# A gated cross-attention block on one core: the last five steps get an instruction order of their own, and TensorE adds the head products of the last tiles

## The chip, the cores and the metric

The kernel runs on one core of a Trainium2 chip. The metric is the device time of one execution in microseconds. Five engines work side by side, each through its own list of instructions in program order, and they wait for each other through semaphores: TensorE (PE, with its weight loads PEld), VectorE (DVE), ScalarE (ACT), GpSimd (POOL) and SyncE (SP), which here only issues transfers.

## What is computed

For 32 sequences of 56 rows with 128 features, in fp32:

```
x = x + tanh(g_xattn) * attention(layernorm(x), ctx[:, :56])   # 16 heads of 64, causal
h  = rmsnorm(layernorm(x)) ; q, k, v per row: 16 heads of 8
att = softmax_g(q[h] . k[g] / sqrt(8))      # among the 16 heads of the same row
y  = layernorm(x) + (att @ v) @ Wo + bo
gate = softmax(rmsnorm(y) @ Wg + bg)        # 8 experts, all are computed
x = x + tanh(g_ffn) * (y + sum_e gate[e] * rmsnorm(y) @ We[e])
```

The causal mask lets no row see beyond key 56, so 56 of the 1500 context rows are used.

## The kernel before

The attention works on 16 pairs of sequences (112 rows). The second half works on 14 tiles of 128 rows, which don't line up with the pairs. A software pipeline of steps `t` joins them: step `t` does the attention of pair `t`, projects a quarter of the queries or keys of a later group (`PROJECT_AT`, steps 2 to 13), and works on up to three tiles: `fa`, whose rows have just become whole, `fb`, one step older, and `fc`, two steps older; POOL adds up the experts of a fourth, `fd`. `TILE_AT` says which tile starts at which step; step 9 starts none. Tile 11 starts in step 14, tile 12 in 15 and tile 13 in 16. There is no attention left from step 16 on, so steps 16, 17 and 18 hold only tiles 11 to 13 (and POOL's sums in step 19).

The order of the instructions on each engine is written out by hand, in one loop per engine (L311 POOL, L443 ACT, L623 DVE, L822 PE). On PE a step is: scores of pair `t` in `ps_b`, `new_y` (output projection of pair `t-1`), `turn_o(fc)`, `shift(t)` (subtracts the row maxima), `new_o(fc)`, four projections, `first(fa)` (tile `fa` into `ps_e`), `turn_x2(fc)`, `values`, `gate_logits(fc)`, `turn_probs(t)`, `expert_half(fc, 0)`, `attend(t)`, `expert_half(fc, 1)`. The expert products, `turn_o`, `new_o` and the gate logits share the two banks of `ps_c`.

Tile `fb` is the work of DVE and POOL: `products` multiplies queries and keys into `prod1` (16 x 16 x 8 values a row, POOL the first `HP` = 10 heads, DVE the other 6), `logits` on DVE adds them over 8 (L529), `shifted_logits` takes maximum and difference, ACT takes exponentials (`head_exps`), `weighted` multiplies them with the values into `prod2` (POOL `HQ` = 6 heads, DVE 10), `mixed_heads` adds over 16 (L554), `normed_heads` scales. For `fc` come `new_x2`, `squares` and `x2_copy` on ACT, gate logits, `gating` on POOL (L304), the expert products scaled on ACT (`experts`, eight instructions of 128 columns, L414), and four additions on POOL (`outputs`, L281 to L289), after which SP stores the tile.

Ahead of everything PE runs seven small products of the identity (L655), while the first loads are under way.

All PE products made through the helper `mm` carry its line, L658. An fp32 product is two MATMUL rows, a transpose or a bf16 product one.

Of the kernel before, what the change touches and what calls it, by code (L numbers as in the profile page):

```python
# [31 lines left out]
WARM_UP = 7  # L32
# [9 lines left out]

def first_step(f):

    return (128 * (f + 1) + T - 1) // T
# [3 lines left out]
LAST_STEP = first_step(NT - 1) + 2  # L49
PROJECT_AT = {t: [("qk"[t % 2], t // 2 + 1, n) for n in range(4)] for t in range(2, NP - 2)}  # L50
# [40 lines left out]
def build(nc, xp, x_t, ctx_t, wq, wk, wv, wo, fw, fup, fdn, fwe, out):  # L91
    with ExitStack() as stack:
# [6 lines left out]
        def sem(name):  # L99
# [89 lines left out]
            o_turned oT_ready o_made x2_ready ssq_ready r2_ready x2_turned x2T_ready  # L189
# [7 lines left out]
        def score_banks(p):  # L197
            return ps_c if p == 1 else ps_b

# [3 lines left out]
        def _(sp):  # L203
# [13 lines left out]
            for f in range(NT):  # L217
                sp.wait_ge(s["out_ready"], f + 1)
                sp.dma_start(out[f * 128:(f + 1) * 128, :], out_sb[f % 2][:, :]).then_inc(stored[f % 2], 16)
# [4 lines left out]
        def _(pool):  # L224
# [31 lines left out]
            def products(f):  # L256
                pool.wait_ge(s["qkv_ready"], f + 1)
                if f > 0:
                    pool.wait_ge(s["logit_ready"], f)
                t = fqkv[f % 2]  # L260
                nc.gpsimd.tensor_tensor(  # L261
                    prod1[:, 0:HP, :, :],
                    t[:, D:2 * D].rearrange("p (g d) -> p g d", g=FH).unsqueeze(1).to_broadcast([128, HP, FH, FD]),
                    t[:, 0:HP * FD].rearrange("p (h d) -> p h d", h=HP).unsqueeze(2).to_broadcast([128, HP, FH, FD]),
                    ALU.mult).then_inc(s["prod1_pool"], 1)

            def weighted(f):
                pool.wait_ge(s["e_ready"], f + 1)
                if f > 0:
                    pool.wait_ge(s["oraw_ready"], f)  # L270
                nc.gpsimd.tensor_tensor(  # L271
                    prod2[:, 0:HQ, :, :],
                    e_sb[f % 2][:, 0:HQ, :].unsqueeze(2).to_broadcast([128, HQ, FD, FH]),
                    fqkv[f % 2][:, 2 * D:3 * D].rearrange("p (d g) -> p d g", d=FD).unsqueeze(1).to_broadcast([128, HQ, FD, FH]),
# [31 lines left out]

            row_scales(0, 2, 1)
# [3 lines left out]
            for t in range(2, LAST_STEP + 2):  # L311
# [3 lines left out]
                if fd is not None:  # L315
                    outputs(fd)
                if fc is not None:
                    second_scale(fc)
                if t < NP:
                    norm(t)  # L320
# [4 lines left out]
                if fc is not None:  # L325
                    gating(fc)

        @block.scalar
        def _(act):
# [64 lines left out]
            def squares(f):  # L394
# [4 lines left out]
                nc.scalar.activation(exb[f % XB][:, E, :], x2[f % 2][:, 0:D], ACT.Copy, scale=gates[:, 2:3])  # L399
# [10 lines left out]
            def experts(f, half):  # L410
                act.wait_ge(s["gate_ready"], f + 1)
                act.wait_ge(s["hi_made" if half else "lo_made"], f + 1)
                for e in range(4 * half, 4 * half + 4):
                    last = nc.scalar.activation(exb[f % XB][:, e, :], ps_c[:, half, e % 4 * D:(e % 4 + 1) * D],  # L414
# [28 lines left out]
            for t in range(2, LAST_STEP + 1):  # L443
# [3 lines left out]
                if t < NP:  # L447
                    exps(t)
                if fc is not None:
                    squares(fc)  # L450
                for fill in PROJECT_AT.get(t, ()):
                    project(*fill)
# [4 lines left out]
                if t < NP:  # L457
                    values(t, 0)
# [10 lines left out]
                if fc is not None:  # L469
                    experts(fc, 0)  # L470
                if fa is not None:
                    kv_copy(fa)
                if fc is not None:
                    experts(fc, 1)

        @block.vector
        def _(dve):
# [40 lines left out]
            def products(f):  # L518
                dve.wait_ge(s["kv_copied"], f + 1)
                nc.vector.tensor_tensor(  # L520
                    prod1[:, HP:FH, :, :],
                    ps_e[:, f % 2, 2 * D:3 * D].rearrange("p (g d) -> p g d", g=FH).unsqueeze(1).to_broadcast([128, FH - HP, FH, FD]),
                    fqkv[f % 2][:, HP * FD:D].rearrange("p (h d) -> p h d", h=FH - HP).unsqueeze(2).to_broadcast([128, FH - HP, FH, FD]),
# [16 lines left out]
            def weighted(f):  # L540
                dve.wait_ge(s["e_ready"], f + 1)
                nc.vector.tensor_reduce(esum[f % 2][:, :], e_sb[f % 2][:, :, :], AX.X, ALU.add).then_inc(s["esum_ready"], 1)
                nc.vector.tensor_tensor(  # L543
                    prod2[:, HQ:FH, :, :],
                    e_sb[f % 2][:, HQ:FH, :].unsqueeze(2).to_broadcast([128, FH - HQ, FD, FH]),
                    ps_e[:, f % 2, 3 * D:4 * D].rearrange("p (d g) -> p d g", d=FD).unsqueeze(1).to_broadcast([128, FH - HQ, FD, FH]),
                    ALU.mult).then_inc(s["prod2_ready"], 1)

            def mixed_heads(f):
                dve.wait_ge(s["esum_ready"], f + 1)  # L550
                nc.vector.reciprocal(einv[f % 2][:, :], esum[f % 2][:, :]).then_inc(s["einv_ready"], 1)
                dve.wait_ge(s["prod2_ready"], f + 1)
# [23 lines left out]
            def gate_sum(f):  # L576
                dve.wait_ge(s["gexp_ready"], f + 1)
                nc.vector.reciprocal(ginv[f % 2][:, :], gsum[f % 2][:, :]).then_inc(s["ginv_ready"], 1)

# [43 lines left out]
            for t in range(2, LAST_STEP + 1):  # L623
# [5 lines left out]
                if t <= NP:  # L629
                    new_x1(t - 1)  # L630
                if fc is not None:
# [4 lines left out]
                if fb is not None:  # L636
                    logits(fb)
# [9 lines left out]
                if fb is not None:  # L647
                    mixed_heads(fb)
                    normed_heads(fb)

        @block.tensor
        def _(pe):
            pe.wait_ge(s["consts"], 2)
            for _n in range(WARM_UP):
                nc.tensor.matmul(ps_b[:, 0, 0:128], ident[:, :], ident[:, :], start=True, stop=True)  # L655
# [92 lines left out]
            def turn_o(f):  # L748
                pe.wait_ge(s["onorm_ready"], f + 1)
                if f > 0:  # L750
# [3 lines left out]
            def new_o(f):  # L754
                if f > 0:
# [142 lines left out]
```

## Time and profile before

| | |
|---|---|
| runs | 275.45, 276.04, 277.45 us; median 276.04 |
| the profiled execution's own time | 274.52 us |
| its span, first to last instruction | 272.5 us |
| PE busy | 240.0 us (88%) |
| DVE, ACT, POOL busy | 193.0, 169.7, 163.9 us |
| TensorE clock, mean granted | 0.947 of 2.4 GHz |

Span and profiled time differ by 2.0 us, which lie around the span. The profiled execution is 1.5 us under the median. In the trace, times are counted from the span's start; the two numbers at the start of a row are its start and its length in us, and what stands in brackets at its end is how long the engine had stood idle before it and what ended that.

### The profile page before, as it was taken

What the parts mean: (1) busy time and instruction counts of PE and PEld (TensorE: products, weight loads), DVE (VectorE), ACT (ScalarE), POOL (GpSimd) and SP (SyncE); (2) the same over time, 40 slices, a digit from 0 to 9 for tenths busy, and PEclk for the clock granted to TensorE, in tenths of its full rate; (3) what the DMA queues carried; (4) which work ended last, traced back from release to release, by engine and by line L of the source; (5) the groups of instructions that cost most, each with busy time, mean ns of one, the idle gap of its engine ahead of it and who ended that gap; (6) DMA issues with size and microseconds to landing.
All of it is one profiled execution on the core that took longest, in us unless ns stands there. A gap on an engine that the chain in (4) does not pass through costs nothing.

```text
span 272.5 us, 7694 instructions
## 1 busy us (share of the span) xinstructions
PE 240.0 (88%) x3146; PEld 169.4 (62%) x3146; DVE 193.0 (71%) x327; ACT 169.7 (62%) x502; POOL 163.9 (60%) x173
## 2 busy tenths in 40 slices
PE   7999979897999999999999999899999797843770
PEld 6765766767676675859585867586857374612320
DVE  0237543479798888888889714998889988998710
ACT  3546516483868768777776767657786555744431
POOL 4104042546476777868684538656877777898544
PEclk9999999999999999999999999999999889996555
DMA  6990000000000000000000000000000000000000
GB/s 196 362 301 9 0 4 2 4 0 5 0 2 10 2 13 4 10 2 12 4 2 10 2 11 2 12 2 0 5 10 2 12 5 11 2 10 10 0 10 10
DMA packets 6016, 7.28 MB, mean 27 GB/s; under 512 B 477, under 2 KB 4830, under 8 KB 5982
## 3 DMA queue, kind: packets, MB, share of 16 engines
q1 hardware_dynamic: 5550, 6.16, 7.1%
q10 hardware_dynamic: 432, 0.64, 0.7%
q8 instruction: 25, 0.41, 0.6%
q14 instruction: 9, 0.07, 0.1%
HBM read 5.88 MB, written 0.92 MB: 25 GB/s over the span
## 4 chain that ended last, share of the span: by engine, by line
PE 65%; ACT 13%; DVE 13%; issue 4%; POOL 2%; DMA 1%; POOLq 0%; SPq 0%; ACTq 0%; DVEq 0%
PE ps_a L658 36%; PE ps_c L658 12%; PE ps_b L658 8%; DVE ps_e L529 5%; ACT probs L359 5%; PE ps_b L710 3%; PE ps_e L658 3%; DVE psums L497 2%; DVE ps_e L554 2%; ACT exb L414 2%; DMA cT<-in_ctx_t 1%; ACT junk L398 1%; ACT qT L342 1%; POOL exb L281 1%; DVE prod L543 1%
## 5 line engine op out<-in xcount | busy, mean ns | idle before, releaser
L261 POOL TENSOR_TENSOR prod<-fqkv 128x1280 f32<-128x1280 f32 x14 | 40.7, 2906 | 3.4 <-DVE fqkv L515 1.9
L658 PE MATMUL ps_c<-fwe_sb,x2T 128*128 128x512 f32 x56 | 34.4, 710 | 5.6 <-DVE glog L571 5.6
L252 POOL TENSOR_TENSOR probs<-probs,prinv 120x672 f32<-120x672 f32 x16 | 22.8, 1427 | 23.8 <-DVE prinv L501 23.7
L414 ACT ACTIVATE exb<-ps_c,gate 128x128 f32<-128x128 f32 x112 | 32.5, 397 | 6.4 <-POOL gate L304 4.2
L658 PE MATMUL ps_a<-aT,wo_sb 128*128 128x112 f32 x256 | 32.9, 281 | 1.0 <-issue 0.6
L658 PEld LDWEIGHTS ps_a<-aT,wo_sb 128*128 128x128 f32 x256 | 29.9, 191 | 3.6 <-issue 1.5
L529 DVE TENSOR_REDUCE ps_e<-prod 128x256 f32<-128x2048 f32 x14 | 32.0, 2286 | 0.0
L281 POOL TENSOR_TENSOR exb<-exb 128x640 f32<-128x640 f32 x14 | 21.6, 1540 | 17.3 <-ACT exb L414 17.3
L554 DVE TENSOR_REDUCE ps_e<-prod 128x128 f32<-128x2048 f32 x14 | 31.3, 2239 | 0.0
L658 PE MATMUL ps_a<-wv_sb,cT 128*64 128x512 f32 x128 | 31.0, 605 | 0.0
L271 POOL TENSOR_TENSOR prod<-e_sb,fqkv 128x768 f32<-128x768 f32 x14 | 25.3, 1810 | 7.2 <-ACT e_sb L387 7.2
L658 PE MATMUL ps_a<-xT,wqc 128*128 128x224 f32 x128 | 27.7, 359 | 1.2 <-ACT qT L342 0.6
L353 ACT COPY aT<-ps_a 128x448 f32<-128x448 f32 x32 | 15.5, 535 | 21.0 <-PE ps_a L658 21.0
L658 PE MATMUL ps_a<-cT,wk_sb 128*128 128x224 f32 x128 | 27.6, 360 | 0.5
L492 DVE TENSOR_REDUCE nmax<-ps_b 120x16 bf16<-120x896 f32 x15 | 16.3, 1086 | 14.0 <-PE ps_b L658 13.9
L658 PEld LDWEIGHTS ps_a<-xT,wqc 128*128 128x128 f32 x128 | 23.1, 190 | 4.8 <-ACT qT L342 3.7
L658 PEld LDWEIGHTS ps_a<-probsT,v_sb 56*64 56x64 f32 x1024 | 17.2, 139 | 13.8 <-ACT probsT L366 12.9
L658 PEld LDWEIGHTS ps_a<-cT,wk_sb 128*128 128x128 f32 x128 | 23.1, 190 | 3.7 <-ACT kT L342 2.8
L342 ACT COPY kT<-ps_a 128x448 f32<-128x448 f32 x32 | 16.9, 530 | 10.5 <-PE ps_a L658 10.3
L497 DVE TENSOR_REDUCE psums<-probs 120x16 f32<-120x896 f32 x16 | 17.4, 1085 | 8.1 <-ACT probs L359 8.1
L658 PE MATMUL ps_a<-probsT,v_sb 56*64 56x56 f32 x1024 | 19.1, 225 | 3.8 <-ACT probsT L366 3.2
L348 ACT COPY v_sb<-ps_a 128x512 f32<-128x512 f32 x32 | 19.2, 598 | 5.3 <-PE ps_a L658 5.3
(122 smaller groups left out, 456.8 us busy)
## 6 DMA issues: line engine op xcount, KB each, us to landing
xp_sb<-in_xp SPq DMA_DIRECT2D x1, 896.0 KB, 8.0
out<-out_sb SPq DMA_DIRECT2D x14, 64.0 KB, 1.5
xT<-in_x_t SPq DMA_DIRECT2D x1, 784.0 KB, 9.5
cT<-in_ctx_t SPq DMA_DIRECT2D x1, 784.0 KB, 11.1
wv_sb<-in_wv SPq DMA_DIRECT2D x1, 512.0 KB, 8.0
wo_sb<-in_wo SPq DMA_DIRECT2D x1, 512.0 KB, 12.2
fwe_sb<-in_fwe SPq DMA_DIRECT2D x1, 512.0 KB, 9.0
fw_sb<-in_fw SPq DMA_DIRECT2D x1, 266.0 KB, 11.7
```

What stands on the lines that cost most here:

```text
L252: nc.gpsimd.tensor_tensor(pr[0:TG, NC:C, :, 0:S], pr[0:TG, NC:C, :, 0:S], prinv[p % 2][0:TG, NC:C, :].unsqueeze(3).to_broadcast([TG, C - N ...
L261: nc.gpsimd.tensor_tensor(prod1[:, 0:HP, :, :], t[:, D:2 * D].rearrange("p (g d) -> p g d", g=FH).unsqueeze(1).to_broadcast([128, HP, FH, ...
L271: nc.gpsimd.tensor_tensor(prod2[:, 0:HQ, :, :], e_sb[f % 2][:, 0:HQ, :].unsqueeze(2).to_broadcast([128, HQ, FD, FH]), fqkv[f % 2][:, 2 * D ...
L281: nc.gpsimd.tensor_tensor(x[:, 0:5, :], x[:, 0:5, :], x[:, 5:10, :], ALU.add).then_inc(s["sum5"], 1)
L342: nc.scalar.copy(dst[:, 2 * k:2 * k + 2, :], ps_a[:, b, 0:2 * GT].rearrange("p (c t) -> p c t", c=2)).then_inc(a_free[b], 1)
L348: nc.scalar.copy(v_sb[p % 2][:, bt, :, :], ps_a[:, b, :].rearrange("p (c d) -> p c d", c=C)).then_inc(a_free[b], 1)
L414: last = nc.scalar.activation(exb[f % XB][:, e, :], ps_c[:, half, e % 4 * D:(e % 4 + 1) * D], ACT.Copy, scale=gate[f % 2][:, e:e + 1])
L492: nc.vector.tensor_reduce(nmax[p % 2][0:TG, :, :], score_banks(p)[0:TG, :, 0:C * S].rearrange("p r (c k) -> p r c k", c=C), AX.X, ALU.max, ...
L497: nc.vector.tensor_reduce(psums[p % 2][0:TG, :, :], probs[p % 2][0:TG, :, :, 0:S], AX.X, ALU.add).then_inc(s["psum_ready"], 1)
L529: nc.vector.tensor_reduce(ps_e[:, f % 2, 0:2 * D].rearrange("p (h g) -> p h g", h=FH), prod1[:, :, :, :], AX.X, ALU.add).then_inc(s["logit ...
L554: nc.vector.tensor_reduce(ps_e[:, f % 2, 0:D].rearrange("p (h d) -> p h d", h=FH), prod2[:, :, :, :], AX.X, ALU.add).then_inc(s["oraw_read ...
L658: return nc.tensor.matmul(o, lhsT, rhs, start=start, stop=stop, skip_group_check=True)
```

## The change

1. The loops end before step 14 (`TAIL`). Steps 14 and 15 get a loop of their own with another order, and steps 16 to 18 are written out for tiles 11, 12 and 13 (`third`, `prior`, `last`).
2. For tiles 10, 11 and 12 PE does the work of `logits`: `logit_sums`, 8 fp32 products of the identity with a slice of `prod1`, 256 columns wide with a stride of 8 values, added up in PSUM. For tile 12 it also does the sum over `prod2`: `head_sums`, 16 products of 128 columns, stride 16. From tile 10 on the heads are shared 8 and 8 in `prod1` and POOL 5, DVE 11 in `prod2`.
3. The expert products of tiles 11 to 13 go to the free banks of `ps_b`, `ps_a`, `ps_b` and no longer wait for the gate logits.
4. The last tile is finished on DVE: gate, four scaled additions straight from PSUM for experts 4 to 7, and three additions, after ACT has scaled experts 0 to 3. POOL adds only the residual.
5. Four small products `stay_warm` on PE behind the gate logits of tile 12.
6. The seven small products at the start become one, 512 columns wide.
7. Steps 2 to 13 are reordered too: DVE does `logits` before `new_x2`, `prob_sums` and `norm`; ACT does the projection copies before `squares`, `head_exps` before both `values` copies, and `experts` 1 before 0; POOL does `norm` before `second_scale`; PE starts the bias half of `new_o` (`bias_o`) ahead of `shift`.

```diff
+TAIL = 14
+END = 16
+HP_LATE = 8
+HQ_LATE = 5
+PE_LOGITS = (10, 11, 12)
+PE_MIXED = (12,)
+BIG = {11: "b", 12: "a", 13: "b"}
+STAY_WARM = 4
@@ pool, steps below 14
-                if fc is not None:
-                    second_scale(fc)
                 if t < NP:
                     norm(t)
+                if fc is not None:
+                    second_scale(fc)
@@ vector
             def products(f):
+                hp = product_heads(f)[0]
                 dve.wait_ge(s["kv_copied"], f + 1)
+                if f - 1 in PE_LOGITS:
+                    dve.wait_ge(s["logit_ready"], f)
...
+            def last_experts(f):
+                x = exb[f % XB]
+                dve.wait_ge(s["last_base"], 1)
+                dve.wait_ge(s["gate_ready"], f + 1)
+                dve.wait_ge(s["hi_made"], f + 1)
+                for e in range(4, E):
+                    if e > 4:
+                        dve.wait_ge(s["last_acc"], e - 4)
+                    nc.vector.scalar_tensor_tensor(out=x[:, E, :], in0=expert_banks(f)[:, 1, (e - 4) * D:(e - 3) * D], scalar=gate[f % 2][:, e:e + 1],
+                                                   in1=x[:, E, :], op0=ALU.mult, op1=ALU.add).then_inc(s["last_acc"], 1)
...
-            for t in range(2, LAST_STEP + 1):
+            for t in range(2, TAIL):
...
+                if fb is not None:
+                    logits(fb)
                 if fc is not None:
                     new_x2(fc)
                 if t < NP:
                     prob_sums(t)
                     norm(t)
                 if fb is not None:
-                    logits(fb)
                     shifted_logits(fb)
...
+            last, prior, third = NT - 1, NT - 2, NT - 3
+            new_x1(NP - 1)
+            products(prior)
+            new_x2(third)
+            shifted_logits(prior)
+            scaled_qkv(last)
+            weighted(prior)
+            products(last)
+            gate_logits(third)
+            head_scales(prior)
+            logits(last)
+            shifted_logits(last)
+            normed_heads(prior)
+            gate_sum(third)
+            weighted(last)
+            new_x2(prior)
+            head_scales(last)
+            head_sums(last)
+            normed_heads(last)
+            gate_logits(prior)
+            gate_sum(prior)
+            new_x2(last)
+            gate_logits(last)
+            gate_sum(last)
+            last_gating(last)
+            last_experts(last)
+            last_sums(last)
@@ tensor
-            for _n in range(WARM_UP):
-                nc.tensor.matmul(ps_b[:, 0, 0:128], ident[:, :], ident[:, :], start=True, stop=True)
+            nc.tensor.matmul(ps_b[:, 0, :], ident[:, :], ident[:, :].unsqueeze(1).to_broadcast([128, 4, 128]), start=True, stop=True)
...
+            def logit_sums(f):
+                pe.wait_ge(s["prod1_ready"], f + 1)
+                pe.wait_ge(s["prod1_pool"], f + 1)
+                for d in range(FD):
+                    ins = mm(ps_e[:, f % 2, 0:2 * D], ident[:, :], prod1[:, :, :, d].rearrange("p h g -> p (h g)"),
+                             start=(d == 0), stop=(d == FD - 1))
+                ins.then_inc(s["logit_ready"], 1)
...
+            for t in range(TAIL, END):
+                fa, fb, fc = TILE_AT.get(t), TILE_AT.get(t - 1), TILE_AT.get(t - 2)
+                scores(t)
+                new_y(t - 1)
+                shift(t)
+                bias_o(fc)
+                turn_o(fc)
+                values(t, 0)
+                new_o(fc)
+                first(fa)
+                turn_x2(fc)
+                if fb in PE_LOGITS:
+                    logit_sums(fb)
+                gate_logits(fc)
+                values(t, 1)
+                turn_probs(t)
+                expert_half(fc, 1)
+                attend(t)
+                expert_half(fc, 0)
+
+            last, prior, third = NT - 1, NT - 2, NT - 3
+            new_y(NP - 1)
+            turn_o(third)
+            bias_o(third)
+            new_o(third)
+            first(last)
+            logit_sums(prior)
+            turn_x2(third)
+            expert_half(third, 1)
+            gate_logits(third)
+            head_sums(prior)
+            bias_o(prior)
+            turn_o(prior)
+            expert_half(third, 0)
+            new_o(prior)
+            turn_x2(prior)
+            expert_half(prior, 0)
+            gate_logits(prior)
+            stay_warm(prior)
+            bias_o(last)
+            turn_o(last)
+            new_o(last)
+            expert_half(prior, 1)
+            turn_x2(last)
+            gate_logits(last)
+            expert_half(last, 0)
+            expert_half(last, 1)
```

## Rows read from the trace of the kernel before

**Rows 1.** The page's slices: granted TensorE clock in tenths, 40 slices

```profile
PEclk9999999999999999999999999999999889996555
```

**Rows 2.** Busy time by stretch: length, then PE, PEld, DVE, ACT, POOL; clock, DMA

```profile
216.50:219.80 3.30, 3.30 (x54) 1.80 (x58) 3.17 (x7) 1.84 (x6) 2.74 (x3) 0.50 0.03 7
...
236.70:247.10 10.40, 4.38 (x18) 2.17 (x17) 9.53 (x16) 5.84 (x26) 9.28 (x11) 1.00 0.02 6
247.10:257.30 10.20, 6.43 (x13) 2.93 (x13) 9.07 (x13) 4.00 (x16) 6.11 (x8) 0.51 0.02 6
257.30:272.50 15.20, 6.46 (x12) 3.02 (x12) 0.90 (x4) 3.91 (x16) 7.20 (x10) 0.50 0.03 9
```

**Rows 3.** The chain that ended last, in a middle step

```profile
78.49 1.14 PE ps_b L658 x68
...
89.90 0.87 PE ps_c L658 x2
...
92.91 0.93 PE ps_b L658 x52
```

**Rows 4.** The timeline of the same step

```profile
82.39 3.58 PE L658 MATMUL ps_a<-cT,wk_sb 128*128 128x224 f32 x16
...
84.19 1.43 PEld L658 LDWEIGHTS ps_a<-cT,wk_sb 128*128 128x128 f32 x8 [0.47 <-ACT kT L342]
...
84.87 1.31 POOL L252 TENSOR_TENSOR probs<-probs,prinv 120x672 f32<-120x672 f32 x1
84.89 2.29 DVE L529 TENSOR_REDUCE ps_e<-prod 128x256 f32<-128x2048 f32 x1
...
88.77 0.90 PEld L710 LDWEIGHTS ps_b<-ident,probs 120*128 120x128 f32 x8
```

**Rows 5.** The timeline of the start

```profile
1.56 3.36 PE L655 MATMUL ps_b<-ident 128*128 128x128 f32 x14 [1.56 <-POOL ident L228]
...
4.96 3.49 PE L658 MATMUL ps_a<-cT,wk_sb 128*128 128x224 f32 x16
...
9.00 0.34 PEld L658 LDWEIGHTS ps_e<-wq_sb,cmat 128*128 128x128 f32 x2 [0.52 <-DMA wq_sb<-in_wq]
```

**Rows 6.** The timeline: where steps 14, 15 and 16 begin on PE

```profile
206.60 0.38 PE L658 MATMUL ps_b<-hide_b,ident_b 56*64 56x448 bf16 x4
...
221.24 0.38 PE L658 MATMUL ps_b<-hide_b,ident_b 56*64 56x448 bf16 x4
...
234.98 2.04 PE L658 MATMUL ps_a<-aT,wo_sb 128*128 128x112 f32 x16
```

**Rows 7.** The timeline of steps 16 to 19

```profile
247.14 0.41 PE L752 MATMUL ps_c<-ident,onorm 128*128 128x128 f32 x1 [3.38 <-DVE onorm L560]
...
252.40 3.78 PE L658 MATMUL ps_c<-fwe_sb,x2T 128*128 128x512 f32 x4 [1.78 <-DVE glog L571]
...
269.98 0.45 POOL L289 TENSOR_TENSOR out_sb<-exb 128x128 f32<-128x128 f32 x1
```

**Rows 8.** Groups of instructions: busy us, mean ns of one, idle before

```profile
L529 DVE TENSOR_REDUCE ps_e<-prod 128x256 f32<-128x2048 f32 x14 | 32.0, 2286 | 0.0
L554 DVE TENSOR_REDUCE ps_e<-prod 128x128 f32<-128x2048 f32 x14 | 31.3, 2239 | 0.0
L520 DVE TENSOR_TENSOR prod<-ps_e,fqkv 128x768 f32<-128x768 f32 x14 | 13.3, 948 | 0.0
L543 DVE TENSOR_TENSOR prod<-e_sb,ps_e 128x1280 f32<-128x1280 f32 x14 | 20.7, 1477 | 0.0
L537 DVE TENSOR_TENSOR ps_e<-ps_e,lmax 128x256 f32<-128x256 f32 x14 | 6.1, 432 | 0.5
L565 DVE SCALAR_TENSOR_TENSOR x<-xc,rstd,ps_c 128x128 f32<-128x128 f32 x14 | 4.9, 348 | 8.1 <-PE ps_c L658 8.1
L414 ACT ACTIVATE exb<-ps_c,gate 128x128 f32<-128x128 f32 x112 | 32.5, 397 | 6.4 <-POOL gate L304 4.2 <-PE ps_c L658 2.2
L281 POOL TENSOR_TENSOR exb<-exb 128x640 f32<-128x640 f32 x14 | 21.6, 1540 | 17.3 <-ACT exb L414 17.3
```

More of the change, by code:

```diff
@@ L326, in _ @@
                     gating(fc)
+            for t in range(TAIL, END):
+                fa, fb, fc, fd = (TILE_AT.get(t - k) for k in range(4))
+                products(fb)
+                outputs(fd)
+                norm(t)
+                second_scale(fc)
+                first_scale(fa)
+                weighted(fb)
+                gating(fc)
+            last, prior, third = NT - 1, NT - 2, NT - 3
+            products(prior)
+            outputs(third - 1)
+            first_scale(last)
+            second_scale(third)
+            weighted(prior)
+            products(last)
+            gating(third)
+            weighted(last)
+            second_scale(prior)
+            outputs(third)
+            gating(prior)
+            second_scale(last)
+            last_residual(last)
+            outputs(prior)
         @block.scalar
@@ L441, in _ @@
             attended(1, 1)
-            for t in range(2, LAST_STEP + 1):
+            for t in range(2, TAIL):
                 fa, fb, fc = (TILE_AT.get(t - k) for k in range(3))
@@ L469, in _ @@
                 if fc is not None:
[L470 removed]
+                    experts(fc, 1)
                 if fa is not None:
@@ L473, in _ @@
                 if fc is not None:
-                    experts(fc, 1)
+                    experts(fc, 0)
+            for t in range(TAIL, END):
+                fa, fb, fc = (TILE_AT.get(t - k) for k in range(3))
+                o_copy(fc)
+                values(t, 0)
+                exps(t)
+                x1_copy(fa)
+                squares(fc)
+                x2_copy(fc)
+                head_exps(fb)
+                values(t, 1)
+                turned_probs(t)
+                gate_exps(fc)
+                attended(t, 0)
+                attended(t, 1)
+                kv_copy(fa)
+                experts(fc, 0)
+                experts(fc, 1)
+            last, prior, third = NT - 1, NT - 2, NT - 3
+            o_copy(third)
+            x1_copy(last)
+            x2_copy(third)
+            squares(third)
+            head_exps(prior)
+            kv_copy(last)
+            gate_exps(third)
+            head_exps(last)
+            o_copy(prior)
+            experts(third, 1)
+            experts(third, 0)
+            squares(prior)
+            x2_copy(prior)
+            o_copy(last)
+            gate_exps(prior)
+            squares(last)
+            x2_copy(last)
+            experts(prior, 1)
+            experts(prior, 0)
+            gate_exps(last)
+            experts(last, 0)
         @block.vector
@@ L621, in _ @@
             nc.vector.tensor_scalar(fwe_sb[:, :, :], fwe_sb[:, :, :], g2_sb[:, 0:1], gates[:, 1:2], ALU.mult, ALU.mult).then_inc(s["experts_scaled"], 1)
-            for t in range(2, LAST_STEP + 1):
+            for t in range(2, TAIL):
                 fa, fb, fc = (TILE_AT.get(t - k) for k in range(3))
@@ L820, in _ @@
             attend(1)
-            for t in range(2, LAST_STEP + 1):
+            for t in range(2, TAIL):
                 fa, fc = TILE_AT.get(t), TILE_AT.get(t - 2)
```

148 lines of the change are left out of this document (116 added, 32 removed).

## The prediction

> **What bounds the kernel now.** I read the page's slices first, then the chain that ended last in a middle step, then its timeline, then the stretches at the end. The slices give the full clock nearly everywhere, a dip near the 31st and a fall in the last four [rows 1]. A middle step lasts 14.4 us from one set of scores to the next (78.49 to 92.91), and its chain is almost all PE [rows 3]: PE bounds steps 2 to 13. Steps 14 and 15 have no projection, which takes 3.4 us of PE's time [rows 4], yet last 14.6 and 13.7 us (206.60, 221.24, 234.98) [rows 6]: there DVE, which must bring the probabilities, the logits and the exponentials in one line, ends last. Of the 14.6, about 1 us is the clock: it was 0.50 from 216.5 to 219.8 [rows 2], when PE had just stood waiting for DVE. From 234.98 to POOL's last addition, which ends at 270.43 [rows 6, 7], three tiles run nearly one behind the other, with DVE busy 9.5 us of 10.4 and 9.1 of 10.2 in the first two rounds, but 0.9 of 15.2 in the last; PE is busy less than half of the time and its clock is 0.50 from 247 on [rows 2]. This tail is 35.4 us.
>
> The sum is made in the profiled execution: 272.5 us of span, 274.52 us in all. The median is 1.5 us above it; I carry the difference over to the median.
>
> **The start.** Fourteen rows of the warm-up take 3.36 us, about 0.24 each, and the sixteen of the keys behind them 3.49 us, 0.218 each for 224 columns [rows 5]. A row of 512 columns at the full clock takes half of 0.87 us, 0.435 [rows 3], which makes 0.11 for 128: so the warm-up ran at half the clock and the keys at the full one. The new product is two rows of 512, 1.7 us at half clock, and then PE stands idle until the first load is in, at 4.96. If the clock is still at half there, as I expect, the cost depends on how long. The stretch at 0.50 in rows 2 lasted 3.3 us of busy PE; such a stretch here costs half of itself, 1.6. All sixteen rows at half clock would cost 2.7 (0.17 more each). The second product of `wq_sb` waited 0.52 us for its load [rows 5], and that cover takes some away. I take +1.0, between 0 and +2.7.
>
> **Steps 2 to 13.** The third projection waits for ACT's copy, which stands behind `squares`; that costs PE 0.06 us a step (82.39 plus half of 3.49 is 84.13, and it starts at 84.19) [rows 4, 5]. Moving the copies forward takes this away, ten times: -0.5. On the other side DVE's `logits`, 2.29 us, now stands ahead of the probability sums and the norm. POOL's norm started at 84.87, after `second_scale`, which now comes behind it. By my walk `logits` runs from 82.1 to 84.4, `new_x2` to 84.7, the sums and reciprocal to 86.1, and the norm on POOL, up to 1.5 us beside DVE's, to 87.7. The transposes of the probabilities start at 88.77 [rows 4], so 1.1 us of cover is left. `squares`, moved behind the copies, hands `x1_copy` on 0.3 us later, and the probability copies start when PE has made them, as before. `new_x2` comes 2.1 us later, with its transposition only 4 us behind the old one on PE; `bias_o` delays the exponentials by 0.2 us, beside the projections. I take -0.5, between -1 and +0.5; if the cover is gone, every late us of the norm is one on PE, in ten steps (a rival below).
>
> **Steps 14 and 15.** DVE loses 2.29 us of `logits` (L529) a step; its share of products grows from 768 to 1024 columns and from 1280 to 1408, 0.3 and 0.15 us more by L520 and L543 [rows 8]; POOL's share shrinks by as much work. PE gains 16 rows of 256 columns. Half a row of 512 is 0.217 [rows 3]; by the key rows with 224 columns it is 0.25 [rows 5]. That is 3.5 to 4.0 us a tile. PE's own work in such a step is 14.4 less 3.4 for the projections, 11.0 at most, and 10.5 if the small gaps of the middle step close: with the sums 14.0 to 15.0. So PE becomes the bound again and fills what DVE leaves. Against 14.6 and 13.7 the two steps give -0.3 to +1.6; I take +0.2, the end without gaps, since PE then never idles long and the 1 us of low clock should go. The added waits of DVE for `logit_ready` of the tile before are met a step early. `values` ahead of `new_o` and the first copy ahead of `exps` hold the exponentials back to 5.5 us into the step; norm and transposes still meet, since `logit_sums` covers PE until 9.5.
>
> **The tail.** Counted from the start of `new_y(15)`: 1.95 us of it, then tile 11's `new_o` behind ACT's last experts, then `first(13)`, and `logit_sums(12)` can start at 3.95 and end near 8.0, ready for DVE. Then DVE has one unbroken line: difference and maximum of tile 12 (0.9), exponentials (0.5), sums and product (2.0), product of tile 13 (1.2), gate and reciprocal (0.6), `logits(13)` 2.3, maximum and difference 0.9, `onorm(12)` and small ones 0.4, sums and product of 13 (2.0), `new_x2(12)` 0.35, reciprocal, L554 2.24, `onorm(13)`: 13.9 us, to 21.9 by the sizes of L529, L554, L520, L543, L537 and L565 [rows 8]. `head_sums(12)` is 32 rows of 128 columns, 3.5 to 4.6 us from 11.4 on, and is done by 16.0, before DVE asks for it at 16.4: nothing. Then, at the full clock, `stay_warm` ends at 22.6; `turn_o`, its copy, `new_o` and `new_x2(13)` take to 24.3; the transposition and gate logits to 25.7. ACT has `squares`, the copy and the eight experts of tile 12 (1.15 us for four, since instructions of 0.397 us overlap [rows 8]) ahead of `gate_exps(13)`: 27.8. Gate 28.2, four chained additions at 0.4 (L565 takes 0.348 [rows 8]) 29.9, three more 30.9. POOL's `outputs(12)` (3.4 us, L281 being 1.54 of it) ends at 30.8, and both stores are issued behind each other, about 0.35 more. That is 31.2 against 35.4: -4.2.
>
> At half clock the two rows of an expert half take 1.9 instead of 0.9 (3.78 for both [rows 7]); `stay_warm` ends at 24.3, `new_x2(13)` at 26.5, and the last high half is only made at 32.5, with DVE's four additions behind it: 35.2, which is -0.2. Which of the two? After `head_sums(12)` ends at 16, PE has 0.9 us of experts, some transpositions, and nothing from 18 to 20.3 but one. In the trace before, the clock fell at 216.5 after a stretch of that kind, but stayed at 1.00 through 236.7 to 247.1, where PE was busy 4.4 us of 10.4 [rows 2]. I take the full clock as a little likelier.
>
> Sum: 1.0 - 0.5 + 0.2 - 4.2 = -3.5, hence 271.0 for the profiled execution and 272.5 for the median.
>
> **The strided reads.** No row here has PE reading a moving operand with a stride; `prod1[:, :, :, d]` steps by 32 bytes, `prod2` by 64. The price of a row lies between the contiguous one and, if each value costs a fetch of its own, a multiple. I take the contiguous one: an fp32 row already takes 0.85 ns a column, 0.435 for 512 [rows 3], two cycles of 0.42 ns at 2.4 GHz, which leaves room for a slower fetch. The Trainium skill, page "SBUF — State Buffer", section "Door 1: The DMA port swizzle", says that SBUF is read in lines of 16 bytes and that each access that crosses into a new line pays; by that rule every column of these sums pays, and no row of the trace shows whether. It speaks against the change, and is the third rival.
>
> **The rivals.**
> (a) The clock falls in the tail: 1.0 - 0.5 + 0.2 - 0.2 = +0.5, 276.5 us. For it: from 247 on it was 0.50 under more scattered work [rows 2]. Against: by my walk no pause of PE is as long as the 3.38 us that stood ahead of 247.14 [rows 7].
> (b) Slower: the strided rows take twice their time. Then `logit_sums` takes 3.5 us more in steps 14 and 15, which PE bounds, so +7; in the tail 3.5 and 3.5 for `head_sums(12)`, of which DVE's line hides 1.3 in all, +5.7. That is 12.7 above the forecast, 285. It turns the sign at 3.5 us over the 80 strided rows, 0.044 each, a fifth of what a row of 256 columns takes. It is what the skill's rule would bring.
> (c) The new order of steps 2 to 13 eats its cover of 1.1 us and 0.3 us more, ten times: +3, 275.5.
> (d) The start costs nothing and the gaps close fully: -5 and more, under 270.
>
> **How the numbers follow.** Forecast 0.47 (its own range 270.3 to 274.3), (a) 0.25, (b) 0.14, (c) 0.08, (d) 0.06. The range 270.0 to 279.0 leaves out (b) and most of (d). About 1%, 2.8 us, is what a measurement of this kernel can tell from no change. Faster by over 1% (under 273.3): 0.43 of the forecast's and (d), 0.49. Slower: (b) and a part of (a) with a dear start, 0.18. Same: 0.33.
>
> **What would show it.** PE's busy share in the new steps 14 and 15 near full with steps of 14.0 to 14.8; the rows of `logit_sums` at 0.22 to 0.25 us; the key rows at the start dearer than 0.218; the clock after `head_sums(12)`; the last expert additions on DVE ending 31 us after `new_y(15)` starts. A clock of 0.50 in the tail, strided rows above 0.26, or middle steps above 14.5 would make me wrong.

## The result, and the profile after

| | before | after |
|---|---|---|
| median (range), us | 275.75 (275.27 to 277.45) | 283.5 (282.6 to 286.35) |
| profiled execution, us | 274.52 | 283.02 |
| span, us | 272.5 | 281.1 |
| TensorE clock, mean granted | 0.947 | 0.986 |

The ratio is 1.029 (1.023 to 1.036): slower by 7.8 us, where I had forecast 3.5 us faster. One execution of the kernel without sums on PE (below) was disturbed and took 474.5 us; medians, ranges and ratios leave it out. TensorE's mean granted clock was higher than before and the kernel still took longer, so a low clock is not what made it slower. The page's slices of after [against rows 1]:

```profile
PEclk9999999999999999999999999999999999997799
```

TensorE's timeline of after, where steps 14, 15 and the tail begin (`hide_b`, then `wo_sb`), and the new sums [against rows 6 and 7]:

```profile
204.39 0.38 PE L831 MATMUL ps_b<-hide_b,ident_b 56*64 56x448 bf16 x4
...
210.41 7.54 PE L831 MATMUL ps_e<-prod,ident 128*128 128x256 f32 x16
217.77 0.30 PE L831 MATMUL ps_c<-fwg_sb,x2T 128*128 128x8 f32 x2
...
222.99 0.38 PE L831 MATMUL ps_b<-hide_b,ident_b 56*64 56x448 bf16 x4
...
229.43 7.53 PE L831 MATMUL ps_e<-prod,ident 128*128 128x256 f32 x16
...
242.07 2.04 PE L831 MATMUL ps_a<-aT,wo_sb 128*128 128x112 f32 x16
...
245.75 7.54 PE L831 MATMUL ps_e<-prod,ident 128*128 128x256 f32 x16
...
256.67 7.33 PE L831 MATMUL ps_e<-prod,ident 128*128 128x128 f32 x32 [1.67 <-DVE prod L639]
...
272.87 1.96 PE L831 MATMUL ps_b<-fwe_sb,x2T 128*128 128x512 f32 x4
```

Cut at the same places, the two traces differ so:

| stretch | before, us | after, us | difference |
|---|---|---|---|
| to the start of step 2 | 36.91 | 39.36 | +2.45 |
| steps 2 to 13 | 169.69 | 165.03 | -4.66 |
| steps 14 and 15 | 28.38 | 37.68 | +9.30 |
| tail, to the end of the last addition | 35.45 | 37.04 | +1.59 |

Up to step 14 after is 2.2 us ahead (+2.45 and -4.66). The loss lies in steps 14 and 15 and the tail, where the sums are: 10.9 us. A `logit_sums` takes 7.54 us, where I had 3.5 to 4.0. A row's length in the trace overlaps the next row, so I count from the first row of the sum to the product behind it (217.77): 7.36 us. A row of 256 columns thus takes 0.46 us, at a granted clock of 1.00 and with PE busy without a gap, as the busy times by stretch show (length, PE, PEld, DVE, ACT, POOL; clock, DMA):

```profile
225.00:240.00 15.00, 15.00 (x70) 8.02 (x72) 7.11 (x13) 5.93 (x21) 7.61 (x9) 1.00 0.02 6
...
256.00:263.00 7.00, 6.33 (x29) 6.33 (x30) 5.36 (x8) 0.78 (x3) 2.57 (x2) 0.51 0.00 0
263.00:270.00 7.00, 5.09 (x26) 3.51 (x25) 5.46 (x10) 3.07 (x13) 4.31 (x5) 1.00 0.00 0
```

In the tail DVE waits for both sums. Its timeline:

```profile
253.33 0.42 DVE L628 TENSOR_REDUCE lmax<-ps_e 128x16 f32<-128x256 f32 x1 [7.46 <-PE ps_e L831]
...
264.04 0.29 DVE L658 TENSOR_TENSOR onorm<-ps_e,einv 128x128 f32<-128x128 f32 x1 [2.15 <-PE ps_e L831]
...
275.15 1.12 DVE L681 TENSOR_SCALAR gate<-gexp,ginv,r 128x8 f32<-128x8 f32 x1
...
278.82 0.29 DVE L704 TENSOR_TENSOR out_sb<-exb 128x128 f32<-128x128 f32 x1
```

The start and a middle step [against rows 5, 3 and 4]; the row at 82.73 is a projection of 16 rows, which took 3.58 us in the same step before:

```profile
1.56 2.07 PE L828 MATMUL ps_b<-ident 128*128 128x512 f32 x2 [1.56 <-POOL ident L246]
5.03 5.87 PE L831 MATMUL ps_a<-cT,wk_sb 128*128 128x224 f32 x16 [1.40 <-DMA cT<-in_ctx_t]
...
42.45 0.92 PE L831 MATMUL ps_a<-aT,wo_sb 128*128 128x112 f32 x6 [0.48 <-issue]
...
78.77 0.38 PE L831 MATMUL ps_b<-hide_b,ident_b 56*64 56x448 bf16 x4
82.73 3.33 PE L831 MATMUL ps_a<-cT,wk_sb 128*128 128x224 f32 x16
88.97 1.02 PE L883 MATMUL ps_b<-ident,probs 120*128 120x120 f32 x8
92.92 0.38 PE L831 MATMUL ps_b<-hide_b,ident_b 56*64 56x448 bf16 x4
```

### The profile page after: what moved, and what is told of

The parts are those of the page before. It is cut to its first block, busy times and chain, and to the rows that moved or that the text cites. A ratio compares the mean times of both kernels' runs of the same rounds, so it can differ in the third digit from the quotient of the medians.

```text
span 281.1 us, 7852 instructions
## 1 busy us (share of the span) xinstructions
PE 261.7 (93%) x3222; PEld 181.8 (65%) x3222; DVE 187.5 (67%) x331; ACT 168.8 (60%) x498; POOL 159.1 (57%) x169
## 4 chain that ended last, share of the span: by engine, by line
PE 80%; ACT 7%; issue 6%; POOL 3%; DVE 2%; DMA 1%; SPq 0%; DVEq 0%; POOLq 0%
PE ps_a L831 45%; PE ps_c L831 11%; PE ps_e L831 10%; PE ps_b L831 8%; PE ps_b L883 4%; ACT exb L464 2%; DMA cT<-in_ctx_t 1%; ACT probsT L416 1%; ACT v_sb L398 1%; POOL prod L279 1%; ACT aT L403 1%; POOL exb L300 1%; DVE exb L692 1%; PE ps_e L918 1%; PE ps_c L927 0%
## 5 line engine op out<-in xcount | busy, mean ns | idle before, releaser
L279 POOL TENSOR_TENSOR prod<-fqkv 128x1280 f32<-128x1280 f32 (+1 forms) x14 | 38.6, 2755 | 1.7 <-DVE fqkv L605 0.7
L831 PE MATMUL ps_e<-prod,ident 128*128 128x256 f32 (+1 forms) x80 | 29.9, 544 | 1.7 <-DVE prod L639 1.7
L831 PE MATMUL ps_a<-cT,wk_sb 128*128 128x224 f32 x128 | 29.4, 384 | 1.4 <-DMA cT<-in_ctx_t 1.4
L652 DVE TENSOR_REDUCE ps_e<-prod 128x128 f32<-128x2048 f32 x13 | 29.3, 2252 | 0.3
L290 POOL TENSOR_TENSOR prod<-e_sb,fqkv 128x768 f32<-128x768 f32 (+1 forms) x14 | 24.3, 1736 | 8.2 <-ACT e_sb L437 8.2
L831 PEld LDWEIGHTS ps_a<-cT,wk_sb 128*128 128x128 f32 x128 | 25.0, 206 | 5.8 <-DMA cT<-in_ctx_t 3.0
L464 ACT ACTIVATE exb<-ps_c,gate 128x128 f32<-128x128 f32 x88 | 25.0, 385 | 1.4 <-PE ps_c L831 1.4
L622 DVE TENSOR_REDUCE ps_e<-prod 128x256 f32<-128x2048 f32 x11 | 25.1, 2285 | 0.4 <-POOL prod L279 0.4
L831 PEld LDWEIGHTS ps_e<-prod,ident 128*128 128x128 f32 x80 | 16.6, 243 | 12.8 <-issue 10.6
L831 PE MATMUL ps_c<-fwe_sb,x2T 128*128 128x512 f32 x44 | 23.7, 621 | 0.0
```

Of the source, the lines that this page charges most:

```text
L279: nc.gpsimd.tensor_tensor(prod1[:, 0:hp, :, :], t[:, D:2 * D].rearrange("p (g d) -> p g d", g=FH).unsqueeze(1).to_broadcast([128, hp, FH, ...
L290: nc.gpsimd.tensor_tensor(prod2[:, 0:hq, :, :], e_sb[f % 2][:, 0:hq, :].unsqueeze(2).to_broadcast([128, hq, FD, FH]), fqkv[f % 2][:, 2 * D ...
L464: last = nc.scalar.activation(exb[f % XB][:, e, :], expert_banks(f)[:, half, e % 4 * D:(e % 4 + 1) * D], ACT.Copy, scale=gate[f % 2][:, e: ...
L622: nc.vector.tensor_reduce(ps_e[:, f % 2, 0:2 * D].rearrange("p (h g) -> p h g", h=FH), prod1[:, :, :, :], AX.X, ALU.add).then_inc(s["logit ...
L652: nc.vector.tensor_reduce(ps_e[:, f % 2, 0:D].rearrange("p (h d) -> p h d", h=FH), prod2[:, :, :, :], AX.X, ALU.add).then_inc(s["oraw_read ...
L831: return nc.tensor.matmul(o, lhsT, rhs, start=start, stop=stop, skip_group_check=True)
```

## The experiments

**What doubles the price of a row?** My theory is the step between the values of the moving operand, the one that streams through PE while the other, the weights, is held (A). The rivals are that sums of identity products into one PSUM bank are slow whatever the step (B), and that DVE or POOL, reading `prod1` at the same time, slow the reads (C). The first kernel appends, behind the last tile, groups of eight identity products that differ in nothing but the step. In effect:

```diff
+            for step in (1, 2, 3, 4, 5, 8, 16, 1):
+                mm(ps_c[:, 0, 128:256], ident[:, :], ident[:, :])
+                src = flat[:, 0:128 * step].rearrange("p (n k) -> p n k", k=step)[:, :, 0]
+                for k in range(8):
+                    mm(ps_c[:, 0, 0:128], ident[:, :], src, start=(k == 0), stop=(k == 7))
+            # then 256 columns with step 1 and 8, and the stepped tensor as loaded weights
```

> The changed kernel with groups of eight identity products added behind the last tile on TensorE; each group reads prod1 with another step (1, 2, 3, 4, 5, 8, 16 values of 4 bytes, then 1 again), 128 columns each; then 256 columns at step 1 and at step 8, then the strided tensor as the loaded weights. The added products are written to a bank that nobody reads, so the output is the same. Theory A, the step of the moving operand sets the price: at full clock about 0.11 to 0.13 us a row at steps 1 and 2, rising between step 4 and step 8 to about 0.22, and 0.46 for 256 columns at step 8 against 0.22 at step 1. Theory B, sums of identity products into one PSUM bank are slow whatever the step: 0.22 and 0.46 at every step. Theory C, VectorE or GpSimd reading prod1 at the same time slows the reads: 0.11 and 0.22 at every step here, since both are nearly done.

It was executed once (314.5 us). TensorE's timeline, a plain product between the groups:

```profile
272.93 1.95 PE L831 MATMUL ps_c<-prod,ident 128*128 128x128 f32 x16
274.72 0.39 PE L831 MATMUL ps_c<-ident 128*128 128x128 f32 x2
274.94 1.98 PE L831 MATMUL ps_c<-prod,ident 128*128 128x128 f32 x16
...
276.98 2.93 PE L831 MATMUL ps_c<-prod,ident 128*128 128x128 f32 x16
...
279.97 3.79 PE L831 MATMUL ps_c<-prod,ident 128*128 128x128 f32 x16
...
287.78 3.89 PE L831 MATMUL ps_c<-prod,ident 128*128 128x128 f32 x16
...
291.73 3.65 PE L831 MATMUL ps_c<-prod,ident 128*128 128x128 f32 x16
...
297.44 3.62 PE L831 MATMUL ps_c<-prod,ident 128*128 128x256 f32 x16
...
301.12 7.54 PE L831 MATMUL ps_c<-prod,ident 128*128 128x256 f32 x16
...
308.72 3.65 PE L831 MATMUL ps_c<-ident,prod 128*128 128x128 f32 x16
```

and the busy times by stretch at its end, in the columns of the stretches above:

```profile
300.00:312.00 12.00, 12.00 (x41) 7.84 (x40) 0.00 (x0) 0.00 (x0) 0.00 (x0) 1.00 0.00 0
```

In the timeline these are steps 1, 2, 3, 4, 8 and 16, then 256 columns at steps 1 and 8, then the loads. From a group's start to the start of the plain product behind it, over 16 rows, a row of 128 fp32 columns takes:

| step, values | 1 | 2 | 3 | 4 | 5 | 8 | 16 |
|---|---|---|---|---|---|---|---|
| us a row | 0.112 | 0.114 | 0.173 | 0.226 | 0.233 | 0.232 | 0.216 |

A holds, though the price rises at steps 3 and 4 already and not between 4 and 8. B falls, since all groups add into one bank in the same way and cost 0.112 at step 1. C falls, since the group of 256 columns at step 8 repeats the 7.54 us of `logit_sums` to the last digit (3.62 at step 1) while DVE, ACT and POOL do nothing. A step of 8 bytes is free, 12 bytes cost one and a half times, 16 to 64 bytes twice. The Trainium skill, page "SBUF — State Buffer", gives two forms of its rule: lines of 16 bytes that want at least two hits each (section "Specifications (TRN2)"), with which the ladder agrees (two hits at step 2, one at step 4), and "4 fp32" as the free step (section "Door 1: The DMA port swizzle"), with which it does not: step 4 took 0.226 against 0.112.

**The same sums with adjacent reads.** The layout of the products of tiles 10 to 12 is turned, so that PE reads adjacent values and DVE and POOL write with the step.

```diff
-                    prod1[:, hp:FH, :, :],
+                    prod1_of(f)[:, hp:FH, :, :],     # tiles 10 to 12: memory order d, h, g instead of h, g, d
...
-                    prod2[:, hq:FH, :, :],
+                    prod2_of(f)[:, hq:FH, :, :],     # tile 12: g, h, d instead of h, d, g
```

> The changed kernel, but prod1 of tiles 10 to 12 and prod2 of tile 12 are laid out so that TensorE reads each slice as adjacent values; VectorE and GpSimd write them with a step instead. Theory A (step of the moving operand): the rows of logit_sums fall from 0.46 to about 0.22 us, steps 14 and 15 become 3.5 us shorter each, the tail 5 us shorter, 271 to 273 us in all. Theory B (identity sums as such): rows stay at 0.46, 283.5 us. Rival D: the writers pay for the step instead, their products (1.22 us on VectorE, 2.35 us on GpSimd) double, and the time ends near 276.

It took 271.9 us (270.8 to 272.7), ratio to before 0.986 (0.980 to 0.993). PE's timeline, and DVE's writers from the groups (busy us, mean ns of one, idle before):

```profile
209.05 3.62 PE L841 MATMUL ps_e<-prod,ident 128*128 128x256 f32 x16
...
217.70 0.38 PE L841 MATMUL ps_b<-hide_b,ident_b 56*64 56x448 bf16 x4
...
232.86 2.04 PE L841 MATMUL ps_a<-aT,wo_sb 128*128 128x112 f32 x16
...
245.22 5.47 PE L841 MATMUL ps_e<-prod,ident 128*128 128x128 f32 x32 [2.60 <-DVE prod L649]
...
262.33 3.69 PE L841 MATMUL ps_b<-fwe_sb,x2T 128*128 128x512 f32 x4
```

```profile
L623 DVE TENSOR_TENSOR prod<-ps_e,fqkv 128x1024 f32<-128x1024 f32 x4 | 7.1, 1765 | 0.0
```

Each sum lost 3.92 us. Steps 14 and 15 lasted 29.83 us (203.03 to 232.86) instead of 37.68, 7.85 less, which is twice 3.92: PE bounds them, and its whole excess is on the path. DVE's products of 1024 columns average 1.77 us, since the three that now write with a step take 1.94 to 1.97 and the fourth 1.20, near the 1.22 of after; the one of `prod2` that writes with a step takes 2.54 for 1408 columns, instead of 1.61. POOL's do not change (2.37 and 1.54 us).

The time came as expected, the tail did not: 35.84 us, only 1.2 less than in after, where I had expected 5 less. Up to the end of `head_sums` it gains 4.1 (250.53 less 232.86 is 17.67, against 21.76 in after). Behind that it loses 2.9 again (18.17 against 15.28), and there the clock is what differs: in this execution it was 0.50 from 256 to 265, where after had 1.00 (the last four expert rows take 3.69 us here and 1.96 there). The busy times by stretch:

```profile
256.00:262.00 6.00, 5.29 (x17) 3.33 (x17) 0.83 (x4) 1.69 (x9) 3.16 (x7) 0.50 0.04 11
```

The execution in the trace took 272.6 us, at a mean clock of 0.972; the fastest of the four took 270.8, at 0.986.

**No sums on PE at all.** DVE adds for tiles 10 to 12 too, with the old shares of the heads; order and tail stay. The shares went back together with the sums, so the two are not told apart.

```diff
-HP_LATE = 8
-HQ_LATE = 5
-PE_LOGITS = (10, 11, 12)
-PE_MIXED = (12,)
+HP_LATE = 10
+HQ_LATE = 6
+PE_LOGITS = ()
+PE_MIXED = ()
...
```

> The changed kernel with no sums on TensorE: VectorE adds prod1 of tiles 10 to 12 right behind its products and prod2 of tile 12 as for the other tiles, heads shared 10/6 and 6/10 as before the change; all else as changed. If the TensorE sums are the whole loss of steps 14 and 15 and more than that of the tail, steps 14 and 15 take 27 to 28.5 us together (37.1 with the sums on TensorE) and the time is 271 to 274 us. If the hand-written order of steps 14 to 18 itself loses, the two steps stay above 30 us and the time above 277.

> The kernel of the run without TensorE sums once more, for a trace at the normal clock. Steps 14 and 15 (scores to scores, then to the last output projection) should take 27 to 28.5 us together, and the tail from there to the last output 33 to 35 us against 35.4 before the change; 270 us in all.

The first time it took 269.9 us (269.6 to 272.4), ratio 0.983 (0.975 to 0.990), the second time 270.4 us (270.05 to 271.3), ratio 0.983 (0.981 to 0.986); the trace is of the second. Steps 14 and 15 took 29.62 us (202.87 to 232.49), as long as with cheap sums on PE and over the 28.5 expected: 3.4 us of them, from 212.9 on, were at a clock of 0.51. The tail took 33.64, as expected, where the adjacent-read sums had 35.84. In time the two kernels are not told apart (0.983 and 0.986, intervals that overlap). So even at the price that I had assumed the sums on PE bring nothing here.

**The start.** The changed kernel with seven small warm-up products again:

```diff
-            nc.tensor.matmul(ps_b[:, 0, :], ident[:, :], ident[:, :].unsqueeze(1).to_broadcast([128, 4, 128]), start=True, stop=True)
+            for _n in range(7):
+                nc.tensor.matmul(ps_b[:, 0, 0:128], ident[:, :], ident[:, :], start=True, stop=True)
```

> The changed kernel with the seven small warm-up products put back. If the single product leaves the clock at half when the keys start, the sixteen key rows go from 5.9 back to 3.5 us and the whole from 283.5 to about 281.1. If the first projection starts late for another reason (its load), nothing changes.

285.7 us (283.3 to 285.8), ratio 1.035 (1.029 to 1.042): I missed, it gained nothing. The keys' rows fell from 5.87 to 4.65 us, but the waits of PE that the trace puts to issue (it shows nothing that PE waits for) are 0.48 and 0.39 us in after, and 1.37, 0.61, 0.21, 0.15, 0.17 and 0.59 here. The reverse, the kernel before with the one wide product as its only edit:

> The kernel before with the single wide warm-up product. In the changed kernel the key rows took 5.9 us instead of 3.5, yet putting the seven products back did not make it faster, since TensorE then waited longer for its instructions in the first steps (2.2 us instead of 0.9). By that the time stays within 1 us of before. If the half clock counts in full, it is 277 to 278.

274.6 us, ratio 0.9965 (0.993 to 0.9996). The keys took 6.25 us and step 2 began at 39.55, 2.64 late, but steps 2 to 13 were 1.42 us shorter (39.55 to 207.82), and of the waits for issue, 2.2 us before, only 0.47 was left. The traces of the two kernels before and with one warm-up, PE's timeline:

```profile
39.51 0.26 PE L658 MATMUL ps_b<-kT,qT 64*56 64x56 f32 x2 [1.37 <-issue]
65.59 1.60 PE L658 MATMUL ps_a<-aT,wo_sb 128*128 128x112 f32 x13 [0.61 <-issue]
```

```profile
4.84 6.25 PE L657 MATMUL ps_a<-cT,wk_sb 128*128 128x224 f32 x16 [1.21 <-DMA cT<-in_ctx_t]
...
42.64 0.92 PE L657 MATMUL ps_a<-aT,wo_sb 128*128 128x112 f32 x6 [0.47 <-issue]
```

The late start is given back; it is no part of the loss. All traces together say the same. Step 2 begins at 36.9 to 38.1 us in the four with seven products and at 38.3 to 39.6 in the nine with one. The waits for issue in steps 2 to 13 add up to 2.2 to 2.9 us in the four, and to 0 to 1.2 in the nine. Why these waits follow the start is open.

**Steps 2 to 13.** The kernel before, with only the new order of these steps; in effect:

```diff
@@ vector, t < 14
+                    logits(fb)
                     new_x2(fc)
                     prob_sums(t)
                     norm(t)
-                    logits(fb)
                     shifted_logits(fb)
```

and the moves of ACT, POOL and PE that go with it.

> The kernel before, with the new order of steps 2 to 13 alone (all four engines); start, steps 14 to 19 as before. In the changed kernel a middle step took 14.15 us instead of 14.42. If the order does it, the sum of ten steps is -2.5 us: 272 to 273 us. If the changed kernel gained there by its later start (less waiting for instructions early on), the time stays near 275.

272.7 us, ratio 0.992 (0.989 to 0.995): the order gains 2.2 us by the ratio. Of the one move to which I had given the whole gain, ACT's `squares` behind the projection copies, the kernel before with it alone says:

> The kernel before, with one edit in steps 4 to 13: ScalarE does squares behind the four projection copies instead of ahead of them. Theory: this alone frees the banks in time, the sixteen projection rows go from 3.43 to 3.16 us and the gain is the same as with the whole new order, 272 to 273 us. Rival: x1_copy and the exponentials behind it come later and steps 14 and 15 or PE's transposes pay: under 1 us gained.

274.2 us, ratio 0.998 (0.994 to 1.001): no gain that is clear of the noise, and not that of the whole order. It shortens a middle step as all moves together do (14.17 us from 79.16 to 93.33, 14.15 in after), but steps 11 to 13 stay at 12.87, 14.76 and 14.73 us, against 12.21, 14.27 and 14.36 with the whole order. Which other move gives those is open.

**What works, put together.** The new order kept through step 15, the tail written out, all sums on DVE. Three variants change its end: the last gate by another form of instruction; no `stay_warm`; and the other form together with the last gate's exponentials ahead of the low experts of tile 12. The edits, against after:

```diff
-TAIL = 14
+TAIL = 16
... the sums on DVE, as above
@@ vector, the other form
-                nc.vector.tensor_scalar(gate[f % 2][:, :], gexp[f % 2][:, :], ginv[f % 2][:, :], r2[f % 2][:, :], ALU.mult, ALU.mult)
+                nc.vector.scalar_tensor_tensor(out=gate[f % 2][:, :], in0=gexp[f % 2][:, :], scalar=ginv[f % 2][:, 0:1],
+                                               in1=r2[f % 2][:, :].to_broadcast([128, E]), op0=ALU.mult, op1=ALU.mult)
@@ scalar, the exponentials ahead
+            gate_exps(last)
             experts(prior, 0)
-            gate_exps(last)
```

> The changed kernel with no sums on PE at all, the new loop order of steps 2 to 13 kept up through step 15, and the hand-written tail with DVE adding (heads shared 10 and 6, 6 and 10 as before). If the parts add up: steps 14 and 15 as in the kernel that had the new loop order alone (27.7 us together), the tail as in the one with all sums on DVE (33.6 us), start and middle steps as there: span 266.3, 268.5 us, 2.5% under the kernel before. If the order written for steps 14 and 15 has a merit of its own without the PE sums, they take 29 us or more here and nothing is gained on 270.4.

> As the kernel with the loop order and the tail on DVE, but the last tile's gate is made by DVE's scalar-tensor-tensor form instead of the tensor-scalar form. If the 1.12 us of the gate (128 x 8 values) come from the form of the instruction beside POOL's 128 x 640 addition, which ended at the same moment, it takes 0.2 to 0.3 us here and the end comes 0.8 us earlier, 267.7. If any DVE instruction would have waited there for POOL, it takes 1.1 us again and the time is the same.

> As the kernel with the loop order and the tail on DVE, but without the four small products behind the gate logits of tile 12. If these raised the clock in the last 12 us, the clock stays at 0.50 to the end here and the tail is 1.5 to 3 us longer (two expert halves at 1.9 instead of 0.9 and the small products), 270 to 271.5. If the clock came back by itself, the time is the same or 1 us less, since the four products stand ahead of tile 13's output projection (8 rows, 1.9 us at half clock).

> As the one with the gate by another form, and ACT makes the last gate's exponentials ahead of the low four experts of tile 12 instead of behind them. ACT's eight experts took from 259.49 to 261.67, while the gate's maximum was there at 260.49: the exponentials come about 0.7 us earlier and the end with them, 267.0. POOL's sum of tile 12 comes 0.4 us later, and ends 0.3 us before the last addition at best: if that takes over the end, half of the gain is lost.

| kernel | median (range), us | ratio to before |
|---|---|---|
| order and tail on DVE | 268.1 (266.8 to 270.6) | 0.976 (0.970 to 0.982) |
| gate in another form | 268.5 (267.3 to 270.1) | 0.975 (0.970 to 0.979) |
| no `stay_warm` | 268.3 (268.2 to 269.7) | 0.975 (0.971 to 0.979) |
| other form, and exponentials first | 266.9 (266.8 to 268.3) | 0.970 (0.966 to 0.974) |

In the kernel with order and tail on DVE, steps 14 and 15 took 26.63 us, shorter than the 27.7 expected, and the tail 33.68, as expected:

```profile
202.92 0.38 PE L834 MATMUL ps_b<-hide_b,ident_b 56*64 56x448 bf16 x4
...
229.55 2.04 PE L834 MATMUL ps_a<-aT,wo_sb 128*128 128x112 f32 x16
```

So the order that the change writes for steps 14 and 15 has no merit of its own: with the sums on DVE the loop's order is 3.0 us shorter (26.63 against 29.62). Up to 1.7 of these are the clock, which in the longer one was 0.51 for 3.4 us. The form of the gate changes nothing: it takes 1.12 us and ends with POOL's addition in both. Here is the other form:

```profile
261.47 1.53 POOL L300 TENSOR_TENSOR exb<-exb 128x640 f32<-128x640 f32 x1 [2.50 <-ACT exb L464]
...
261.90 1.12 DVE L681 SCALAR_TENSOR_TENSOR gate<-gexp,ginv,r 128x8 f32<-128x8 f32 x1
```

Where it comes before POOL's addition, in the last kernel of the table, it takes 0.23:

```profile
258.36 0.23 DVE L681 SCALAR_TENSOR_TENSOR gate<-gexp,ginv,r 128x8 f32<-128x8 f32 x1
259.20 1.51 DVE L692 SCALAR_TENSOR_TENSOR exb<-ps_b,gate,exb 128x128 f32<-128x128 f32 x4 [0.61 <-PE ps_b L834]
259.23 1.54 POOL L300 TENSOR_TENSOR exb<-exb 128x640 f32<-128x640 f32 x1 [1.83 <-ACT exb L464]
...
261.08 0.70 DVE L700 TENSOR_TENSOR exb<-exb 128x128 f32<-128x128 f32 x1
```

In that trace the tail is 0.7 us shorter (32.96 against 33.68), as expected, and POOL's sum of tile 12 now ends last, 0.4 us behind DVE's last addition. In time the gain over the first kernel of the table is not clear of the noise: the intervals overlap, and the two profiled executions took 267.1 us each. Moving the exponentials alone was not tried. Leaving `stay_warm` out costs nothing that can be measured.

## Why the prediction was wrong

**The step that failed** is the one under "The strided reads": "I take the contiguous one". At the full clock the row costs twice that, 0.46 us for 256 columns against 0.22 with adjacent values. My reason, that two cycles a column leave room for a slower fetch, covers only a step of 2 values by the ladder; the kernel steps by 8 and 16. The right answer stood among the rivals, (b) (that section calls it the third), as 285 us for the median; it was 283.5. Its two parts: +7 in steps 14 and 15, measured 7.85 between the kernels with stepped and with adjacent reads; and +5.7 in the tail, of which those two kernels show 1.2 (37.04 against 35.84). The 1.2 is not the price of the step. Of the 4.1 that adjacent reads gain up to the end of `head_sums`, the low clock of that execution takes 2.9 back. The rest of the way to 5.7 is that the adjacent reads were bought with dearer DVE writes, and that `head_sums` ran at half clock for most of its rows, where the step costs nothing: 0.229 us a row in after, as the warm-up's rows of the same width at half clock, 0.24 [rows 5].

**The start**, +1.0 (0 to +2.7): measured +2.45 in this pair of executions; over all traces the nine with one product begin step 2 on average 1.4 us behind the four with seven, so the term was well sized. That the clock would still be low when the keys start was right (5.87 us for their rows, of which I had put the dearest case at 3.49 and 2.7). What I did not see is that it is given back.

**Steps 2 to 13**, -0.5 (-1 to +0.5): measured -4.66 in the profiled execution. The later start gives 1.4 of it (168.27 us with the old order and one product, 169.69 before). The order gives the other 3.2 (165.03 against 168.27); with seven products it gives 2.3 (167.43 against 169.69), and that trace has 2.0 us more of waits for issue than after. So I had mis-sized this term too: the sixteen projection rows of the middle step fell from 3.58 to 3.33 us, where I had taken 0.06 a step. The feared loss of cover (c) did not come: the transposes of the probabilities began 10.2 us into the step (78.77 to 88.97), before 10.3.

**Steps 14 and 15**, +0.2 (-0.3 to +1.6): that PE becomes the bound and fills what DVE leaves was right, "with the sums 14.0 to 15.0" a step nearly so with adjacent reads (14.67 and 15.16), +1.45 over before and inside the range. What I left out is that taking DVE's 2.29 us off was not worth it: the same steps with DVE's sums were as long in this order and shorter in the loop's.

**The tail**, -4.2, or -0.2 at half clock: with adjacent reads it was +0.4. The half clock came there (0.50 from 256 to 265 us), so rival (a), which I had put below the full clock, describes that tail better: DVE's line started 8.1 us into it, as forecast (8.0), took 14.9 (forecast 13.9), and the rest took 12.9, where the forecast had 9.3 at full and 13.3 at half clock. In after, DVE could start its line 11.3 us into the tail (forecast 8.0), that line took 15.8 us (forecast 13.9; the 2.15 us wait for `head_sums`, which I had at nothing, are in it), and the rest 10.0 (forecast 9.3, with the gate at 0.4 instead of 1.12). The four chained additions were right, 1.51 us for 1.6.

With my own assumption made true, the kernel took 271.9 us, where the forecast was 272.5. That is luck. Against my terms its profiled execution shows +1.2 at the start (step 2 at 39.08), +1.3 in steps 14 and 15 and +4.6 in the tail, and -5.2 in steps 2 to 13 (163.95 us against 169.69): large misses that cancel.

## What to carry to other kernels

Before a sum or a gather is given to TensorE as identity products, write down the step in bytes of the operand that it reads: here, at the full clock, fp32 rows cost nothing extra up to 8 bytes and double from 16 to 64. Turning the layout moves the price to the writer, so it must be added there. And price the step of an engine by what is freed on the others: work moved from DVE to a PE without gaps is paid in full, and only an order that lets both run, as in steps 2 to 15 here, gives time back.

## What the runs showed of the hardware

- TensorE, fp32 moving operand, full clock: 0.112 us for 128 adjacent columns, 0.114 at step 2, 0.173 at 3, 0.226 at 4, 0.216 at 16. At half clock step 16 took 0.229, adjacent values 0.24. The same tensor as loaded weights, step 16: 3.65 us for 16 loads and products, against 1.95 for the group with adjacent values.
- DVE writing each next value 1 KB further: 1.94 us instead of 1.22 for 1024 columns, 1.6 times; each next value 512 bytes further: 2.54 instead of 1.61 for 1408. POOL with the same pattern: 2.37, unchanged.
- Some DVE instructions whose inputs lie all in SBUF waited for POOL's addition: the gate of 128 x 8 values took 1.12 us and ended with POOL's in two forms, 0.23 without it, and an addition of 128 columns 0.70 instead of 0.29. Four with an input in PSUM took 1.51 us together, whether beside POOL's 640 columns or its smaller additions. A reduction of 8 values and a reciprocal of 16, both reading SBUF, did not wait: 0.16 and 0.24 us in after, beside POOL's product of 1024 columns, and 0.16 and 0.25 without it. The Trainium skill, page "SBUF — State Buffer", section "Terms", describes such a port pair, locked for a whole instruction; the rows that waited agree.
- The clock in the tail: in after it fell at 256, when PE had just stood idle (0.01 of 1 us busy, and 1.67 us of waiting before `head_sums`), stayed at 0.50 through nearly all of the 32 rows that followed without a gap, and was 1.00 from 263 on. Of the last four kernels it came back at 254 in the first, after `stay_warm` had begun at 252, near 257 in the one without `stay_warm`, and only after 263 in the one with the gate in another form, which has it.
